# A hybrid layer on one core: the first FFN's routing of each token group moved into attention a's rounds

## What is computed

```python
x = x + _L0_attn_a_ref(_layernorm(x, axis=-1), ...)
x = x + _L0_ffn_ref(_layernorm(x, axis=-1), ...)
x = x + _L0_attn_b_ref(_layernorm(x, axis=-1), ...)
x = x + _L0_ffn_ref(_layernorm(x, axis=-1), ...)

def _L0_ffn_ref(input_features, centroids, ln_g, ln_b, w1, b1, w2, b2):
    x = input_features.reshape(-1, Df)
    aff = x @ centroids.T
    assign = jnp.argmax(aff, axis=1)
    order = jnp.argsort(assign)
    ...
    alpha = jax.nn.sigmoid(jnp.take_along_axis(aff[order], es[:, None], axis=1))
    for e in range(nE):
        h = _layernorm(xs, ln_g[e], ln_b[e])
        h = jax.nn.relu(h @ w1[e].T + b1[e])
        ye = xs + h @ w2[e].T + b2[e]
        y = y + jnp.where((es == e)[:, None], ye, 0.0)
    out_sorted = alpha * y + (1.0 - alpha) * xs
```

## Time and profile before

| | |
|---|---|
| three runs | 563.9, 565.84, 568.18 us; median 565.84 |
| the profiled execution | 566.51 us, its span 564.7 us |
| mean granted TensorE clock | 0.905 |
| PE / DVE / ACT / POOL busy | 461.5 (82%) / 374.8 (66%) / 228.8 (41%) / 235.9 (42%) us |
| attention a's rounds | 50 to 92 us of the span |
| routing up to the first FFN matmul | 92 to 134 us |

### The profile page before, as it was taken

How to read it: one execution, slowest core, us unless ns; L and a number is a source line. 1 busy time by engine, 2 the same in 40 slices (tenths; PEclk the granted TensorE clock), 3 DMA queues, 4 the chain that set the end, 5 groups by cost and what they waited for, 6 DMA issues and landing times.

```text
span 564.7 us, 10428 instructions
## 1 busy us (share of the span) xinstructions
PE 461.5 (82%) x3500; PEld 362.5 (64%) x3500; DVE 374.8 (66%) x1091; ACT 228.8 (41%) x835; POOL 235.9 (42%) x245
## 2 busy tenths in 40 slices
PE   3957895715989179999999999999999997419993
PEld 2324554614989046777787877878787785319993
DVE  6598976851666347767768687696777955345772
ACT  2720001501444006555646466366564564104451
POOL 5002784471444314433435334363444624322453
PEclk9987998555999669999999999999999999758998
DMA  8999600034464200000000000000000000116560
GB/s 296 403 422 420 277 1 1 15 109 136 142 176 148 77 1 2 1 1 2 1 1 2 2 1 11 11 20 1 2 11 11 21 0 1 39 62 178 155 201 19
DMA packets 21878, 47.73 MB, mean 85 GB/s; under 512 B 3233, under 2 KB 13480, under 8 KB 19394
## 3 DMA queue, kind: packets, MB, share of 16 engines
q1 hardware_dynamic: 18818, 40.73, 20.7%
q0 software_dynamic: 3008, 6.34, 3.3%
HBM read 23.82 MB, written 24.15 MB: 85 GB/s over the span
## 4 chain that ended last, share of the span: by engine, by line
PE 69%; DVE 10%; POOL 8%; DMA 5%; issue 5%; ACT 2%; POOLq 0%; SPq 0%; ACTq 0%; DVEq 0%
PE ps L888 10%; PE ps L917 9%; PE ps L964 8%; PE ps L951 7%; PE ps L833 7%; PE ps L846 6%; PE ps L905 5%; PE ps L895 5%; PE ps L923 3%; POOL sum L441 3%; DMA pv<-in_w 2%; POOL sorted_in L466 2%; PE ps L681 2%; POOL sum L445 2%; PE ps L787 1%
## 5 line engine op out<-in xcount | busy, mean ns | idle before, releaser
L495 POOL TENSOR_TENSOR vT<-vT,prec 128x256 f32<-128x256 f32 (+1 forms) x128 | 103.1, 825 | 157.5 <-DVE prec L1373 157.4
L632 ACT ACTIVATE vT<-ps,nmax 128x128 f32<-128x128 f32 (+1 forms) x256 | 105.1, 434 | 27.8 <-DVE nmax L1365 27.8
L640 ACT COPY prod<-ps 128x384 f32<-128x384 f32 x96 | 42.9, 481 | 111.3 <-PE ps L951 108.3
L1365 DVE TENSOR_REDUCE nmax<-ps 128x2 f32<-128x256 f32 (+1 forms) x128 | 62.3, 548 | 25.6 <-PE ps L923 25.6
L888 PE MATMUL ps<-xnT,wb 128*128 128x256 f32 x256 | 67.9, 389 | 4.6 <-DVE xnT L1345 3.9
L951 PEld LDWEIGHTS ps<-cst,vT 128*128 128x128 f32 x384 | 44.7, 140 | 18.8 <-issue 14.5
L632 ACT ACTIVATION_READ_ACCUMULATOR vT<-ps,nmax 128x1 f32 x256 | 55.9, 218 | 0.0
L951 PE MATMUL ps<-cst,vT 128*128 128x128 f32 x384 | 52.5, 273 | 1.8 <-POOL vT L495 1.7
L888 PEld LDWEIGHTS ps<-xnT,wb 128*128 128x128 f32 x256 | 44.8, 195 | 10.8 <-DVE xnT L1345 4.3
L917 PE MATMUL ps<-qk 64*128 64x128 f32 (+1 forms) x512 | 51.2, 339 | 0.0
L964 PE MATMUL ps<-prod 128*64 128x256 f32 (+1 forms) x512 | 50.0, 338 | 1.4 <-ACT prod L640 1.4
(11 more groups left out here) (152 smaller groups left out, 829.8 us busy)
## 6 DMA issues: line engine op xcount, KB each, us to landing
sorted_in<-zero SPq DMA_DIRECT2D x1, 16512.0 KB, 59.2
pv<-in_w SPq DMA_DIRECT2D x30, 259.0 KB, 2.8
pv<-sorted_in SPq DMA_DIRECT2D x46, 129.0 KB, 2.5
wps<-in_w SPq DMA_DIRECT2D x1, 2072.0 KB, 10.1
w2s<-in_w SPq DMA_DIRECT2D x1, 2048.0 KB, 13.8
wb<-in_w_b SPq DMA_DIRECT2D x1, 1536.0 KB, 18.0
xres<-in_x SPq DMA_DIRECT2D x4, 256.0 KB, 3.6
xres<-after_ffn SPq DMA_DIRECT2D x4, 256.0 KB, 3.8
```

Source lines behind the costliest of these rows:

```text
L495: last = nc.gpsimd.tensor_tensor(px, px, view(prec, m_at(n, x) + t * 2, [[1, 2], [0, (t + 1) * P]]), ALU.mult)
L632: last = nc.scalar.activation(pb[:, o:o + (t + 1) * P], wide[:, c:c + (t + 1) * P], ACT.Exp, bias=nmax[:, m:m + 1], accum_out=psum[:, m:m ...
L640: nc.scalar.copy(pT[:, c:c + BLOCKS * P], bank[hh][:, 0:BLOCKS * P]).then_inc(b_pa, 1)
L1365: last = nc.vector.tensor_reduce(nmax[:, m:m + 2], view(wide, x * 1024 + t * P, [[512, 2], [1, (t + 1) * P]]), AX.X, ALU.max, negate=True)
```

## The change

The routing of a group moves up into the rounds. VectorE does `residual_a`, `means` and `spread` of group 0 after round 3 and of group 1 after round 5; `norm(0, 0)` after round 4; `choose` and `count` of group 0 after round 5; `place(0, 0)` and `norm(0, 1)` after round 6; the rest in an interleaved order after round 7. TensorE, ScalarE and GpSimd follow in the same order. The last round is no longer added up by GpSimd: `out_a(7)` takes all ten slots of each of its two halves straight from `pv`, twenty matmuls in place of eight. PSUM places of the transposed tiles, affinities and ranks are other ones (`turned_at`, `aff_at`, `rank_at`), and two of `out_a`'s banks wait for their readers.

```diff
+        turned_at = ((0, 512, 0, 512), (6 * 512,) * NG)
+        aff_at = ((0, 4 * 512, 5 * 512, 4 * 512), (5 * 512, 5 * 512, 5 * 512, 2 * 512))
+        rank_at = ((512, 6 * 512, 7 * 512, 3 * 512), (5 * 512, 5 * 512, 5 * 512, 3 * 512))
...
-            for r in range(NR):
-                add_up(r)
...
+            for r in range(NR - 1):
+                add_up(r)
+                if r in (3, 5):
+                    powers(0, r // 2 - 1)
+            powers(0, 2)
             pool.wait_ge(filled, 16)
-            for g in range(NG):
-                powers(0, g)
-            for g in range(NG):
+            dispatch(0, 0)
+            powers(0, 3)
+            for g in range(1, NG):
                 dispatch(0, g)
...
-                pe.wait_ge(a_sum, r + 1)
+                summed = r < NR - 1
+                if summed:
+                    pe.wait_ge(a_sum, r + 1)
                 pe.wait_ge(a_pv, 3 * r + 3)
                 if k % 2 == 0:
                     need(pe, a_x, r // 2 - 1)
+                    if r == 4:
+                        pe.wait_ge(f_oh, 1)
+                    if r == 6:
+                        pe.wait_ge(f_vTs, 2)
...
+                if i == 17:
+                    pe.wait_ge(in_r, 1)
+                    pe.wait_ge(in_f, 4 * 16)
+                    turn_v(0, 0)
+                if i == 18:
+                    affinity(0, 0)
+                if i == 21:
+                    rank(0, 0)
+                    out_a(4)
+            out_a(5)
+            pe.wait_ge(f_row, 1)
+            turn_v(0, 1)
+            pe.wait_ge(a_pv, 3 * NR - 2)
+            affinity(0, 1)
+            out_a(6)
+            out_a(7)
+            turn_v(0, 2)
+            rank(0, 1)
+            affinity(0, 2)
+            turn_v(0, 3)
+            rank(0, 2)
+            affinity(0, 3)
+            rank(0, 3)
+            totals(0)
...
+            def residual_ffn(u):
+                residual_a(u)
+                dve.wait_ge(a_x, u + 1)
+                means(0, u)
+                spread(u)
...
+            for r in range(NR):
+                for c in range(3):
+                    weigh_values(3 * r + c)
...
+                if r == 3:
+                    residual_ffn(0)
+                if r == 4:
+                    norm(0, 0)
+                if r == 5:
+                    residual_ffn(1)
+                    choose(0, 0)
+                    count(0, 0)
+                if r == 6:
+                    place(0, 0)
+                    norm(0, 1)
+            residual_ffn(2)
+            choose(0, 1)
+            count(0, 1)
+            norm(0, 2)
+            residual_ffn(3)
+            place(0, 1)
+            norm(0, 3)
```

More of the change, by code:

```diff
@@ L579, in turned_v @@
                 need(act, f_aff, n)
-                nc.scalar.copy(vTt[:], bank[k][:]).then_inc(f_vTs, 1)
+                nc.scalar.copy(vTt[:], wide[:, turned_at[k][g]:turned_at[k][g] + GT * P]).then_inc(f_vTs, 1)
             def exps(k, g):
@@ L615, in ffn @@
                         normed(s + 2)
[L617 to L622, removed]
+            for g in range(2):
+                turned_v(0, g)
+                residual(0, g)
+                exps(0, g)
+            for g in range(2, NG):
+                turned_v(0, g)
+                residual(0, g)
+            for g in range(2, NG):
+                exps(0, g)
             act.wait_ge(in_f, 4 * 16)
@@ L738, in out_a @@
                     q = (r % RP * 2 + j) * 2 * P
-                    slots = [sum2[:, q + s * P:q + (s + 1) * P] for s in range(2)]
-                    for s in range(8, rest(t) + 1):
+                    slots = [sum2[:, q + s * P:q + (s + 1) * P] for s in range(2 if summed else 0)]
+                    for s in range(8 if summed else 0, rest(t) + 1):
                         c = (r % RP * 2 + j) * SLOTS * P + s * P
@@ L765, in _ @@
             pe.wait_ge(a_qkv, 3 * NU)
[L766 to L773, removed]
             def turn_v(k, g):
@@ L779, in turn_v @@
                     t = g * GT + i
-                    last = nc.tensor.transpose(bank[k][:, i * P:(i + 1) * P], pack[:, t * ROW:t * ROW + D], ident)
+                    at = turned_at[k][g] + i * P
+                    last = nc.tensor.transpose(wide[:, at:at + P], pack[:, t * ROW:t * ROW + D], ident)
                 last.then_inc(f_vT, 1)
@@ L816, in totals @@
                 last.then_inc(f_total, 1)
+            for i in range(3 * NR):
+                expand(i)
+                if i == 8:
+                    out_a(0)
+                    total(1)
+                if i in (11, 14, 17):
+                    out_a(i // 3 - 2)
+                if i == 17:
[22 more added lines that the diff above has]
+            totals(0)
             def ffn(k):
@@ L861, in ffn @@
                 output(NSLOT - 1)
[L863 to L872, removed]
             ffn(0)
@@ L1267, in tables @@
                                                  ALU.mult))
+            def residual_ffn(u):
[3 more added lines that the diff above has]
+                spread(u)
+            nc.vector.tensor_copy(view(pack, 2 * D + 1, [[ROW, NT]]), cst[:, C_TOKEN:C_TOKEN + NT])
+            for r in range(NR):
+                for c in range(3):
+                    weigh_values(3 * r + c)
+                if r == 1:
+                    differences(1)
+                if r == 2:
+                    weights(1)
+                if r == 3:
[16 more added lines that the diff above has]
+            norm(0, 3)
+            choose(0, 2)
+            count(0, 2)
+            place(0, 2)
+            choose(0, 3)
+            count(0, 3)
+            place(0, 3)
+            tables(0)
             def ffn(k):
@@ L1306, in ffn @@
                 finish(NSLOT - 1)
[L1308 to L1324, removed]
             ffn(0)
```

12 lines of the change are left out of this document (removed).

## The result

| | before | after |
|---|---|---|
| median of 20 runs | 565.58 us (563.12 to 569.57) | 572.66 us (568.15 to 578.49) |
| the profiled execution, its span | 566.51, 564.7 us | 569.03, 567.2 us |
| mean granted clock | 0.905 | 0.915 |
| last send ends, counted from the residual of group 0 | 60.99 us | 63.62 us |

The ratio is 1.0097 (95% interval 1.0073 to 1.0122), about 5.5 us slower, or 571.1 us. It is taken without the two longest runs of the changed kernel, which were in a slower state; the quotient of the medians is higher, 1.0125 with those two and 1.0122 without them (6.9 us). The forecast was 1.0 us slower, in a range that ended at 571.5. From here on the **mark** is the end of the sixteenth send less the start of the residual of group 0 (before 129.92 - 68.93 = 60.99), since executions reach that residual at 66.8 to 68.9 us for reasons ahead of the change.

The account below looks back on a forecast made before the run. GpSimd's sixteen issues were taken as the bound from 109.73; the full-clock schedule ended 1.3 us earlier (128.6), but the clock's fall and group 2's late alpha made it 130.9, +1.0: 566.8 us, range 561.0 to 571.5.

Parts of the forecast that it names:

- What bounds the kernel: Tail of the routing: GpSimd's sixteen indirect DMA issues from 109.73, about 1.26 us each; twelve left after the change, 15.2 us.
- The turn-taking: Rounds 4 to 7: VectorE's moved SBUF instructions wait for GpSimd's additions, up to 2.35 us each time, 1.27 more meeting L445.
- The faster rival: Rounds 4 to 7: GpSimd's additions hardly hold VectorE's moved pieces; -7.8 to -4.0 us, chance 0.13.
- the schedule without it: Same schedule without any holding: rounds end at 102.1, issues at 122.1, against 128.6 with holding at full clock.
- The rule on the shared port: Moved choose during GpSimd's powers: by the page held, end 1.0 us later, at +2.0; the sum took it as bare.
- TensorE's sum of round 7: out_a(7): twenty matmuls, 5.0 us, replace GpSimd's addition and eight matmuls; 5.5 us against 5.8, worth 0.3 us alone.
- The clock: TensorE falls to 0.50 once, back by about 94 or 96; costs 1.8 us on the path, issues end at 130.9.
- the hole: TensorE idle between its last chunk before round 6 (85.2) and the next (90.5), 5.3 us, making the clock fall.
- the slower rival's case: Clock falls again or stays low during out_a(5) to out_a(7): +2.8 us, chance 0.2; above +5.7, up to +15, chance 0.1.
- Group 2's alpha: Before group 2's issues: comes 0.7 us late because rank and affinity run at clock 0.50 as before.
- the fastest case: No holding of VectorE by GpSimd: issues end at 122.1, or 125.9 with one fall of the clock; chance 0.13.
- the premise that what follows the mark is only shifted: After the last issue (129.92 before): the same program, started earlier or later, so its difference is added to the median.

Follow-up runs that it names:

- e3: GpSimd's additions cut to a few columns (leaves out nearly all of the sum), in the changed kernel 565.23 us, 0.9973, and in the kernel before 566.48 us, 0.9985.
- e2: Kernel before with only TensorE's sum of round 7 added (twenty matmuls in out_a(7)): 570.99 us, ratio 1.0063, mark 63.37 us.
- e1: Changed kernel with GpSimd adding up round 7 again, eight matmuls in out_a(7): 569.71 us, ratio 1.0056 to the kernel before, mark 60.90 us.
- e0: The changed kernel once more, no edit: 570.69 us, ratio 1.0078 to the kernel before, mark 64.90 us.
- e4: Changed kernel with six extra matmuls in TensorE's idle stretch before round 7's first chunk, two jobs: 563.21 and 568.81 us, ratios 0.9958 and 1.0038.
- e5: Kernel before with only means (with its residuals) moved into the rounds: 564.13 us, ratio 0.9948, mark 55.84 us.
- e7: Kernel before with means in the rounds, groups served one by one, and ten unread matmuls before TensorE's wait for sorted tokens: 564.30 us, ratio 0.9952.
- e8: Kernel before with fifteen unread matmuls between TensorE's last rank and its wait for sorted tokens: 567.39 us, ratio 0.9981.

## Why the prediction was right, and where it wasn't

**The whole**: the time came out slower, as forecast, and within the range, but the size was missed: 5.5 us for 1.0. By the ratio it is 571.1 us and the range ended at 571.5; by the median, 572.7, it would be outside. That it lies inside is owed to the width of the range, which was set by the scatter of the runs, and, so close to its end, to luck. The mechanism is judged below by the mark.

**What bounds the kernel**: right. The end is set by the sends on GpSimd, and the twelve that are left pace themselves at 1.26 us as before.

**The turn-taking**: right, in kind and mostly in size. Rounds 4 to 7 were put at 4.0, 11.7, 20.3 and 28.3 us behind residual 0 and came at 3.66, 10.87, 19.17 and 28.23. The faster rival (holding hardly bites) is refuted by the held rows and by e3. The price of all the holding was put too high: the schedule without it ended 6.5 us earlier (122.1 for 128.6), and e3 gives 3.6 to 4.9 us. The prediction also spoke only of rows with both operands in SBUF, and two others were held: L1185 (1.19 us, bare 0.17) and the cast L1239 (0.94, bare 0.17), which have one tensor operand.

**The rule on the shared port**: the prediction went by the row and not by the Trainium skill ("SBUF — State Buffer", section "SBUF: two separate sides"), by which the moved `choose` would be held by the powers. After shows L1215 of that `choose`, both operands in SBUF, at 102.48 and bare, 0.19 us, inside the powers of 102.21 to 103.86: the measurement decides against the page here.

**TensorE's sum of round 7**: this step failed. "So this part alone is worth 0.3 us" compared 5.5 us of matmuls with 5.8 us of addition and matmuls, "if it is free". It isn't free: before, TensorE made the rest of `out_a(5)`, the bias and `out_a(6)` while GpSimd added, and only eight matmuls stood behind. In e2 the twenty stand behind `out_a(6)`, and the part costs 2.4 us. The schedule of the forecast had them in a row (3.04 and 5.0), so the mark didn't suffer from it, but the text called a loss a small gain.

**The clock**: the hole was expected at 5.3 us and was 4.70; the clock was expected back 25 to 27 us behind residual 0 and came back 27.8 behind it (95.5). The forecast took one fall; both profiles of the changed kernel have two, as have those of e1 and of e3 in this order, which is the slower rival's case (+2.8; measured +2.6, with +3.9 in e0). The second fall lies where that rival put it. The page "TensorE: Matmul & The Clock Gate", Part 4, of the Trainium skill had made that second fall likelier by its rule on transposes. But both profiles of e4 have the same transposes in the same place and no second fall, so the transposes alone don't bring it about. What does isn't shown; the two profiles without it are the two in which the clock was at 1.00 from 87.2 on. That the hole goes with the first fall holds for the first profile; in e0 and in the first profile of e4 the clock fell at 80.3, some 5 us before the last chunk ahead of the hole was done. Two sums of the rivals don't follow from their terms: 12 us more on 130.9 end at 142.9 (+13), not 145 (+15), and one fall is priced at 2.3 us in the forecast and at 3.8 in the fastest case (122.1 to 125.9).

**Group 2's alpha**: the gap was put at 0.7 us and was 1.25 - 0.30 = 0.95, for another reason: ScalarE's timeline in after has `exps` (L587) behind the four L575 of the same group:

```profile
118.51 1.65 ACT L575 ACTIVATE pack<-xres,shift,plus 128x128 f32<-128x128 f32 x4
120.06 0.19 ACT L587 ACTIVATE ea<-arg 128x4 f32<-128x4 f32 x1
```

**The size**: the mark explains 2.6 to 3.9 us of 5.5 (interval 4.1 to 6.9) and of 4.4 us. The rest isn't settled. Even that much rests on the premise that what follows the mark is only shifted: counted from residual 0, the first FFN's last store was issued 1.3 us later than before in the first profile and 2.9 in e0, less than the mark in both. In the first pair of spans, counted from their starts, the first FFN ends at the same time (its last store at 186.6 in both), and the 2.5 us lie in the second one, whose stores run from 514.66 to 559.58 against 514.98 to 557.01. That length varies from 42.0 to 46.0 us among all profiles here, also among kernels that differ in nothing there, so no cause is read from it. Over the thirteen rows of the table, time and mark differ by -4.1 to +3.6 us.

## What to carry to other kernels

Before moving work into another engine's idle time, ask what its neighbour does in that time: here the move gained 5.2 us at the mark for the instructions that aren't held (e5), and nothing where held ones were moved with them (e1, -0.1). A sum moved from an engine that works beside the others to the one that comes last lengthens the path, even if it looks shorter (2.4 us in e2). And where a change is worth 1 to 3 us of 566, judge it by a mark close to it in several profiles; the median of one job can be off by more than that.

## What the runs showed that was not expected

- The same kernel, e4, took 563.21 us in one job and 568.81 in another, on another chip, each against its own runs of the kernel before (567.3 and 567.4).
- Ten or fifteen matmuls bring TensorE back to its full clock within a wait, but it fell again after they had ended (ended at 126.46 and fell at 129.7 in e7, 130.53 and 133.7 in e8), with the real work already under way.
- VectorE stood still for 4.83 us in one execution with its operands made and no releaser that the profile names; the cause is open.
- A held row lasts to the end of the addition in which it started: L1195 lasted 1.87 us, the two behind it started before the second addition (76.31) and ran bare, and L1199, which started inside it, lasted 1.16. But not every row with its operands in SBUF is held: inside one addition (89.41 to 91.75) the TENSOR_REDUCE L1238 ran bare, 0.19 us, and the cast L1239 behind it was held to the end.
